# Two preactivated 3x3 convolutions on eight images: units of 12 rows of two images in 64x64 tiles against blocks of 16 rows of one image in 64x32 and 32x32 tiles

## The reference

```python
def _gn(v, G=4, eps=1e-5):           # group norm: 4 groups of 2 channels, whole image
    g = v.reshape(B_, G, C_ // G, H_, W_)
    m = jnp.mean(g, axis=(2, 3, 4), keepdims=True)
    s = jnp.var(g, axis=(2, 3, 4), keepdims=True)
    return ((g - m) / jnp.sqrt(s + eps)).reshape(v.shape)

# x: (8 images, 8 channels, 1024, 1024) fp32; weights (8, 8, 3, 3), bias (8,)
x = x + conv3x3(_gn(x), L0_conv_weight) + L0_conv_bias     # layer 0
x = x + conv3x3(_gn(x), L1_conv_weight) + L1_conv_bias     # layer 1
return x
```

## Time and profile before

| | |
|---|---|
| median of three runs | 4156.16 us |
| span of the profiled execution, first to last instruction | 4141.6 us |
| matmuls (PE) busy | 3666.7 us, 89% |
| weight loads (PEld) busy | 1715.4 us, 41% |
| DVE / ACT / POOL busy | 2025.6 / 1762.8 / 1360.0 us |
| moved by DMA | 1435.04 MB, mean 346 GB/s |
| granted clock of PE, mean | 0.983 |

### The profile page before, as it was taken

How to read it: one execution, slowest core, us unless ns; L and a number is a source line. 1 busy time by engine, 2 the same in 40 slices (tenths; PEclk the granted TensorE clock), 3 DMA queues, 4 the chain that set the end, 5 groups by cost and what they waited for, 6 DMA issues and landing times.

```text
span 4141.6 us, 88712 instructions
## 1 busy us (share of the span) xinstructions
PE 3666.7 (89%) x33232; PEld 1715.4 (41%) x33232; DVE 2025.6 (49%) x3110; ACT 1762.8 (43%) x1381; POOL 1360.0 (33%) x1829
## 2 busy tenths in 40 slices
PE   0087777898889999999888999999999999999999
PEld 0032222353334433354333443345444444566665
DVE  6866666665556344446656444444445322232222
ACT  0032222343334555543333555544443555555554
POOL 0011111121112555531111455552111455555555
PEclk9999998999999999999999999999999999999999
DMA  9989999999999999999999999999999999999997
GB/s 333 396 291 393 386 374 371 366 368 387 382 382 331 331 367 385 380 318 391 390 388 384 305 357 371 374 295 368 362 355 333 291 306 306 306 287 304 305 303 237
DMA packets 367109, 1435.04 MB, mean 346 GB/s; under 512 B 49888, under 2 KB 50016, under 8 KB 334176
## 3 DMA queue, kind: packets, MB, share of 16 engines
q10 hardware_dynamic: 176736, 627.30, 47.9%
q0 software_dynamic: 153344, 536.96, 34.5%
q1 hardware_dynamic: 36864, 268.45, 16.9%
HBM read 895.64 MB, written 536.87 MB: 346 GB/s over the span
## 4 chain that ended last, share of the span: by engine, by line
PE 56%; DMA 15%; ACTq 11%; issue 10%; DVE 5%; ACT 2%; DVEq 0%; POOL 0%; POOLq 0%; SPq 0%
PE conv L653 56%; DMA out_dram<-out_tile 12%; ACTq L479 11%; DMA stat_tile<-x_dram 2%; DVE bn_x L700 2%; ACT out_tile L465 1%; DVE bn_mid L710 1%; DMA mid_dram<-out_tile 1%; DVE out_tile L727 1%; DVE mv_mid L738 1%; DVEq L700 0%; DVE mv_x L732 0%; PE conv L555 0%; ACTq L461 0%; PE conv L583 0%
## 5 line engine op out<-in xcount | busy, mean ns | idle before, releaser
L653 PE MATMUL conv<-x_tile,wts 64*64 64x512 f32 x32832 | 3648.7, 598 | 235.5 <-ACT out_tile L465 140.4
L653 PEld LDWEIGHTS conv<-x_tile,wts 64*64 64x64 f32 x32832 | 1694.9, 134 | 2170.3 <-issue 2037.0
L465 ACT ACTIVATE out_tile<-conv,bias 128x1024 f32<-128x1024 f32 x688 | 728.6, 1110 | 1340.5 <-PE conv L653 791.1
L710 DVE BATCH_NORM_STATS2 bn_mid<-out_tile 128x512 f32 (+1 forms) x1376 | 849.3, 680 | 881.1 <-ACT out_tile L465 880.9
L727 DVE TENSOR_SCALAR out_tile<-conv,bias 128x1024 f32<-128x1024 f32 x340 | 436.4, 1284 | 1168.7 <-PE conv L653 856.7
L371 POOL DMA_DIRECT2D mid_dram<-out_tile x680 | 343.4, 507 | 1708.1 <-ACT out_tile L465 1641.4
L470 ACT ACTIVATE out_tile<-conv,bias 128x1024 f32<-128x1024 f32 x344 | 383.1, 1114 | 764.4 <-PE conv L653 505.6
L508 ACT ACTIVATE x_tile<-x_tile 16x2048 f32<-16x2048 f32 x340 | 648.6, 1908 | 44.9 <-issue 31.6
L700 DVE BATCH_NORM_STATS2 bn_x<-stat_tile 128x512 f32 (+1 forms) x1024 | 628.7, 678 | 45.6 <-DMA stat_tile<-x_dram 45.5
L405 POOL COPY x_tile<-x_tile 16x2048 f32<-16x2048 f32 x340 | 639.1, 1880 | 1.7
L385 POOL DMA_DIRECT2D out_dram<-out_tile x680 | 348.3, 514 | 823.7 <-DVE out_tile L727 758.8
(11 more groups left out here) (62 smaller groups left out, 114.5 us busy)
## 6 DMA issues: line engine op xcount, KB each, us to landing
x_tile<-x_dram ACTq DMA_DIRECT2D x680, 512.0 KB, 23.0
stat_tile<-x_dram SPq DMA_DIRECT2D x256, 1024.0 KB, 9.8
out_dram<-out_tile POOLq DMA_DIRECT2D x680, 384.0 KB, 7.8
mid_dram<-out_tile POOLq DMA_DIRECT2D x672, 384.0 KB, 9.3
x_tile<-mid_dram ACTq DMA_DIRECT2D x340, 640.0 KB, 6.4
x_tile<-mid_dram ACTq DMA_DIRECT2D x344, 128.0 KB, 8.5
mid_dram<-out_tile POOLq DMA_DIRECT2D x8, 416.0 KB, 10.0
x_tile<-x_dram ACTq DMA_DIRECT2D x8, 256.0 KB
```

Source lines behind the costliest of these rows:

```text
L465: last = act.activation(out_tile[0:parts, slot, i], conv[0:parts, bank, i], ACT.Identity, bias=bias0[0:parts, win.parity, int(unit.last), ...
L653: last = nc.tensor.matmul(to, weights, x_tile[HALF * half:HALF * (half + 1), slot, middle, c + kw:c + kw + BANK], start=(kw == 0), stop=(k ...
L710: last = dve.bn_stats(bn_mid[0:parts, unit.win.pair % 2, i, bass.ds(unit.n * 2 + h, 1), :] .rearrange("p a b -> p (a b)"), out_tile[0:part ...
```

## The change

The whole kernel body is written anew for another tiling.

* A *block* is 16 rows of one image, 16 rows x 8 channels = 128 partitions, and each input row is loaded once. A *unit* is two blocks (32 rows of one image), 32 units to a *pass* (one layer of one image), 16 passes: 512 units.
* The input block is shifted by one row against the output block (input rows 16b+1 to 16b+16 for output rows 16b to 16b+15). Four quarters of 4 output rows each (32 partitions) make up the output block. Two of them need only rows of one half of the input block: `whole`, a 64x32 tile. The other two need rows of two quarters: `split`, two 32x32 tiles, the upper of which may lie in the block before.
* A unit is 2 column halves x 3 `kw` x (4 `whole` + 8 `split`) = 72 matmuls of 512 columns. The 12 of one `kw` cover the array once.
* Passes run in plain order: layer 0 of image n, layer 1 of image n, layer 0 of image n+1. The sums of a pass are made between two passes, with one set of weights.
* ACT makes all evictions (one of 128 partitions and two of 64 for each unit, since the second block's halves are swapped in PSUM) and asks for rows behind them, for the units 3 and 4 on. There are 8 slots of one block each. At the fourth unit from a pass's end it also asks for a small transfer of padding rows and waits for it.
* No halos are copied, DVE evicts nothing, and POOL stores only (two transfers of 512 KB to a unit).
* The statistics of x are those of the next image, asked for by SP as units get done.

```diff
-PAIRS = IMAGES // 2
-RING = 4
-X_RING = 8
-ROWS_IN = 8
-ROWS_OUT = 6
+TILE = P // 4
+BLOCKS = SIDE // ROWS
+UNITS = BLOCKS // 2
+TRIP = 4
+TRIPS = UNITS // TRIP
+SLOTS = 2 * TRIP
+PASSES = 2 * IMAGES
...
+            def whole(parity, j, c, kw):
+                for i in range(2):
+                    for h in range(2):
+                        part = slice(HALF * h, HALF * (h + 1))
+                        nc.tensor.matmul(columns_of(parity, i, 2 * h + 1, c), wts[part, WHOLE, kw],
+                                         rows_of(HALF * h, HALF, 2 * j + i, c, kw),
+                                         start=(kw == 0), stop=(kw == KW - 1))
+
+            def split(parity, j, c, kw):
+                first, end = c == 0 and kw == 0, c == 1 and kw == KW - 1
+                for i in range(2):
+                    slot = 2 * j + i
+                    for h in range(2):
+                        part = slice(HALF * h, HALF * h + TILE)
+                        nc.tensor.matmul(columns_of(parity, i, 2 * h, c), wts[part, SPLIT, kw],
+                                         rows_of(HALF * h, TILE, slot, c, kw), start=first, stop=end)
+                        q = 1 if h else 3
+                        part = slice(TILE * q, TILE * (q + 1))
+                        above = slot if h else (slot - 1) % SLOTS
+                        last = nc.tensor.matmul(columns_of(parity, i, 2 * h, 1 - c),
+                                                wts[part, SPLIT, kw],
+                                                rows_of(TILE * q, TILE, above, 1 - c, kw),
+                                                start=first, stop=end)
+                return last
...
+                whole(parity, j, 0, 0)
+                split(parity, j, 0, 0)
+                whole(parity, j, 0, 1)
+                split(parity, j, 0, 1)
+                whole(parity, j, 0, 2)
+                split(parity, j, 0, 2).then_inc(half_added, 1)
+                whole(parity, j, 1, 0)
+                pe.wait_ge(half_added, UNITS * p + TRIP * t + (j + 1))
...
+            with pe.Fori(0, PASSES) as p:
+                sums(p)
+                pe.wait_ge(pads_written, p + 1)
+                pe.wait_ge(wts_ready, p + 1)
...
+            def load_last_pad(layer, n):
+                act.wait_ge(pad_row_filled, 2 * n + (layer + 1))
+                act.sem_inc(rows_asked)
+                act.dma_start(x_tile[P - CH:P, LAST_SLOT, 1:SIDE + 1], pad_row[0:CH, :]) \
+                    .then_inc(last_pad_loaded, 16)
...
+                if (g + TRIP - 1) % UNITS == UNITS - 1:
+                    load_last_pad(layer, n)
+                    load(TRIP, 0)
+                    act.wait_ge(last_pad_loaded, 32 * n + 16 * (layer + 1))
+                    act.sem_inc(rows_asked)
+                    load(TRIP - 1, 1)
                 else:
+                    load(TRIP - 1, 1)
+                    load(TRIP, 0)
...
+                act.activation(out_tile[:, slot, 0], conv[:, parity, 0], ACT.Identity,
+                               bias=bias[:, 0:1]).then_inc(evicted, 1)
+                act.activation(out_tile[HALF:P, slot, 1], conv[0:HALF, parity, 1], ACT.Identity,
+                               bias=bias[0:HALF, 0:1]).then_inc(evicted, 1)
+                act.activation(out_tile[0:HALF, slot, 1], conv[HALF:P, parity, 1], ACT.Identity,
+                               bias=bias[HALF:P, 0:1]).then_inc(evicted, 1)
+                load_next(n, g, last_image)
```

More of the change, by code:

```diff
@@ L11 @@
 P = 128
-HALF = P // 2
 CH = 8
@@ L156, in last_stores @@
[L156 to L169, removed]
+PER_GROUP = STATS * STAT_PARTS // GROUPS
+MID_PARTS = UNITS * 2 * HALVES
+STAT_UNITS = sorted(list(range(0, 60, 2)) + [31, 33])
@@ new lines, in image @@
+            def image(n, first_image=False, last_image=False):
+                for layer in range(2):
+                    act.wait_ge(var_read, 2 * n + (layer + 1))
+                    act.activation(root[:, :], var[:, :], ACT.Sqrt).then_inc(root_done, 1)
+                    act.wait_ge(wts_ready, 2 * n + (layer + 1))
+                    for u in range(UNITS):
+                        evict(n, layer * UNITS + u, first_image, last_image)
+            load_head(0, 0)
+            for b in range(LAST_SLOT):
+                load_block(0, 0, b)
@@ L549, in _ @@
+            image(0, first_image=True)
+            with act.Fori(1, IMAGES - 1) as n:
+                image(n)
+            image(IMAGES - 1, last_image=True)
         @block.tensor
         def _(pe):
-            def mean_sum(n, bank):
-                pe.wait_ge(mean_share, n + 1)
-                regions = 1 if WINDOWS[n].layer == 0 else 3
-                for region in range(regions):
-                    last = nc.tensor.matmul(conv[:, bank, 1, BANK:BANK + BOTH], average[:, :],
-                                            share[:, region], start=(region == 0),
-                                            stop=(region == regions - 1))
-                last.then_inc(mean_summed, 1)
@@ L560, in var_sum @@
-            def var_sum(n, bank):
-                pe.wait_ge(var_share, n + 1)
-                regions = 1 if WINDOWS[n].layer == 0 else 3
-                for region in range(regions):
-                    last = nc.tensor.matmul(conv[:, bank, 1, BANK:BANK + BOTH], average[:, :],
-                                            share[:, region], start=(region == 0),
-                                            stop=(region == regions - 1))
-                last.then_inc(var_summed, 1)
-            def own(i):
-                return slice(VALID * i, VALID * i + HALF)
@@ new lines, in rows_of, with columns_of @@
+            def rows_of(first, rows, slot, c, kw):
+                at = c * BANK + kw
+                return x_tile[first:first + rows, slot, at:at + BANK]
+            def columns_of(parity, i, quarter, c):
+                column = TILE * ((quarter + 2 * i) % 4)
+                return conv[column:column + TILE, parity, i, c * BANK:(c + 1) * BANK]
+            def whole(parity, j, c, kw):
+                for i in range(2):
+                    for h in range(2):
+                        part = slice(HALF * h, HALF * (h + 1))
+                        nc.tensor.matmul(columns_of(parity, i, 2 * h + 1, c), wts[part, WHOLE, kw],
+                                         rows_of(HALF * h, HALF, 2 * j + i, c, kw),
+                                         start=(kw == 0), stop=(kw == KW - 1))
@@ L854, in _, with make_bias @@
-            dve.memset(rows0[:, 0:KW, :], 0.0)
-            after_all(dve.memset(rows1[:, :, :, :], 0.0))
+                dve.wait_ge(head_loaded, 16 * (p + 1))
+                dve.tensor_scalar(x_tile[part, LAST_SLOT, 1:SIDE + 1], head[part, :],
+                                  is_first[part, 0:1], above[part, 0:1], ALU.mult, ALU.add) \
+                   .then_inc(pads_written, 1)
+            def make_bias(p, layer):
+                dve.wait_ge(bias_summed, p + 1)
+                dve.tensor_scalar(bias[:, :], conv[:, 0, 0, GROUPS:GROUPS + 1],
+                                  bias_col[:, layer:layer + 1], None, ALU.add).then_inc(wts_ready, 1)
@@ L949, in _taps @@
+            with dve.Fori(0, IMAGES - 1) as n:
+                image(n, False)
+            image(IMAGES - 1, True)
 def _taps(weight, np):
```

969 lines of the change are left out of this document (313 added, 656 removed).

## The result

The kernel after took **6574.1 us**, the kernel before 4156.5 us beside it (medians of four runs each): the ratio is 1.582, with a 95% interval from 1.5781 to 1.5861. One of the four runs after, 7669 us at a mean granted clock of 0.793, was disturbed and is left out of the ratio. The profiled execution took 6573.2 us, with a span of 6571.5. The forecast was 3761 us. The case that came true is rival 1, for which 6000 us were worked out.

A forecast was written before the change was run, and what follows sets the result against it. Half the kernel was taken as DMA-bound, half as PE-bound, with DMA the limit after: 127 start + 3452 DMA + 109 boundaries + 48 padding + 10 end = 3746 us span, plus 15 makes 3761 us; range 3560 to 4150.

The forecast's parts named there:

- rival 1: Tiles of two sizes do not run side by side on PE; a unit takes 10.4 to 11.6 us, 6000 us in all; 17%.
- Can the 12 tiles fill it?: PE's instruction pace: 144 record pairs must come in 5.2 us, 36 ns each; bounds 4.2 and 8.0 us a unit.
- PE's work: Conv matmuls: 512 units of 6 array covers at 5.21 us, 2668 us against 3584 before, 916 us less.
- the warm row: PE's warm stream before the change: 36 pairs of one column at 29 ns each, taken as the nearest price.
- The two records of another size: Beside the 128x128 sums on PE, two records of 8 columns push the next unit by 0.31 us, some 0.1 us a switch.
- Bytes: DMA traffic: 1342 MB against 1435, as the halo rows of layer 0 go.
- Start: First pass: one image's sums, aggregations and the chain to the first conv matmul; conv starts at 127 us, 228 before.
- ACT: Three evictions and two requests take 3.3 to 4.4 us of a unit, below 6.9, so no bound; costed at nothing.
- DMA's rate: Mixed traffic when DMA is the limit: 378 GB/s, weighted from four stretches at 369 to 388.
- Boundaries: Between passes PE idles 15.7 us (layer 0 to 1) or 8 us (1 to 0); DMA loses 109 us in all.
- The padding row: ACT's wait for a small transfer in each pass: 3 us of idle DMA in each of 16, 48 us; upper bound 160.
- The sum: The whole span: start, DMA-paced passes, boundaries, padding waits and end make 3746 us, plus 15 is 3761 us.

The follow-up runs named there:

- twelve tiles: The kernel with all tiles 32x32, but 12 of the 16 of each `kw`, half of each `whole` left out (another output): 3826.3 us.
- the last kernel: All tiles 32x32, ACT's image loop unrolled, DVE writes the padding row into the slot in place of the small transfer: 3853.5 us, ratio 0.9235 to the kernel before.
- experiment (c): On all tiles 32x32: padding transfer waited for one unit later, ACT's image loop unrolled, GpSimd fills the padding row after the weights: 3906.0 us, ratio 0.9364.
- (b): On the kernel with all tiles 32x32, ACT's loop over the images is unrolled: 3926.7 us, ratio 0.9416.

## Why the prediction was wrong

**The step that failed** is "Can the 12 tiles fill it?", and with it "*PE's work*": "512 units of 6 covers, if `whole` and `split` fill the array together". They do not. The forecast of PE's unit was 5.21 us, it took 12.06, and 512 x 6.85 = 3507 us are more than the whole miss of 2813 (DMA's waits, which the forecast had, are hidden behind PE now). The step looked for the price of a pair of instructions, between 29 and 56 ns, and took the warm row. That part held: with one size a `kw` of 24 pairs takes 0.86 us, 36 ns a pair, and one of 32 pairs 1.05, 33 ns. But all rows of overlap are of one size, and the sum went by them. The two records of another size spoke of 0.1 us for a change. The Trainium skill (TensorEngine Tiling (Array Packing), Key Properties), which rival 1 quotes, says that a change of the tiling mode drains the engine. Both pointed at rival 1, which got 17%.

**Rival 1** named the mechanism and undersized it: 6 x 1.74 = 10.4 us is right (10.31), a change is 0.146 us and not 0.1, so a unit is 12.06 and not 11.6. Over its upper end, 6280, that is 512 x 0.46 = 236 us. The 15 boundaries are 437 - 15 x 12.06 = 256 us instead of 190, 66 more. Together 6582. For 224 of the 256 us no conv matmul runs; the other 32 are the first units, 2 us too long each. In the first pass of layer 1 the granted clock is 0.50 (the 1.2 GHz level) for PE's first 5 us, from 533.6 to 538.6, after 17.8 us in which it had run the few matmuls of the sums only. No term of the sum had that. The signs that it named are all there: PE busy throughout, `whole` and `split` in groups, DMA at 216 to 220 GB/s.

The other steps, the second half of them by the kernels with equal tiles, as DMA isn't the limit after:

* *Bytes*: 1342 forecast, 1344.3 measured.
* *Start*: conv at 127 us. Its first matmul starts at 127.3, with 32x32 tiles at 125.0. Right.
* *ACT* at nothing: right. In the kernel after it idles 8.7 us in each unit, with 32x32 tiles 3.34, ended by PE both times.
* *DMA's rate*, 378 GB/s: 381 and 384 in the last kernel's stretches. Right for these, but it isn't the same whatever the mix: with twelve tiles the passes of layer 0 move 381 to 388 GB/s and those of layer 1 394 to 398, while layer 0 of the last image, which reads no statistics, has a share of 1.02 at 345.
* *Boundaries*: 15.7 us without PE from layer 0 to 1. Here they are in the timeline of the kernel after; the last eviction of the pass began at 515.9.

```profile
519.35 1.29 DVE L476 BATCH_NORM_STATS2 bn_mid<-out_tile 128x6 f32<-128x512 f32 x2 [0.98 <-ACT out_tile L341]
520.79 3.62 DVE L490 BATCH_NORM_AGGREGATE mv_mid<-bn_mid 128x2 f32<-128x768 f32 x1 [0.15 <-DVE bn_mid L476]
524.82 0.56 PE L367 MATMUL conv<-share,average 128*128 128x4 f32 x2 [9.00 <-DVE share L492]
...
528.07 2.90 POOL L243 TENSOR_SCALAR pad_row<-zeros,own_mean 8x1024 f32<-8x1024 f32 x1 [7.50 <-DVE own_mean L525]
528.22 0.99 DVE L531 TENSOR_SCALAR newton<-newton 128x4 f32<-128x4 f32 x1
...
530.01 1.08 DVE L541 TENSOR_SCALAR wts<-band,own_rstd 128x192 f32<-128x192 f32 x1
...
533.64 1.93 PE L395 MATMUL conv<-x_tile,wts 64*32 64x512 f32 x8 [2.55 <-DVE bias L562]
```

It took 17.7 us. Statistics (1.3) and aggregation (3.6) are as forecast; of the 2 us more, 1.5 are in the chain behind, where two of DVE's small instructions take 0.8 us longer beside GpSimd's fill (L243). With the fill moved behind the weights, experiment (c), the same instructions are short:

```profile
373.94 0.16 DVE L537 TENSOR_SCALAR newton<-newton 128x4 f32<-128x4 f32 x1
374.91 0.32 DVE L547 TENSOR_SCALAR wts<-band,own_rstd 128x192 f32<-128x192 f32 x1
...
377.13 2.83 POOL L243 TENSOR_SCALAR pad_row<-zeros,own_mean 8x1024 f32<-8x1024 f32 x1 [10.83 <-DVE bias L568]
```

From layer 1 to 0 PE stands for 8.2 to 8.3 us where ACT doesn't jump, as forecast. The jump of ACT's loop, 4 to 7 us at each of five of these boundaries, was in no term.
* *The padding row*: 3 us in each of 16 passes, 48 in all. With 32x32 tiles it is 8 to 10 us in the last three units of seven passes of layer 0 and none in the other nine. From (b) to the last kernel, which has no such wait, the passes are 56 us shorter together and the boundaries 10 (the fill is gone too). The total is near by luck: the price of a pass was too low by a factor of about three, and nine of the 16 passes pay nothing.
* *The sum*: the change as it was meant, with equal tiles and free of ACT's wait, its jump and the fill, has a span of 3855 us against 3746. It adds up as 128 at the start, 512 x 6.72 = 3441, 15 boundaries of 323 - 15 x 6.72 = 222, 55 of units over 6.72 and 10 at the end. The unit of 6.72 holds the pause at the wait for `half_added`, which no term had; what it would be without that wait wasn't run. The forecast had 109 for the boundaries, because PE at 5.2 us a unit would catch up what DMA's queue held ready. At 6.72 us PE has nothing to catch up with, and the boundaries count in full. That reading comes from the sum, no run tests it alone.

## What to carry to other kernels

Tiles of two sizes did not share TensorE's array in either pair tried, on columns of their own: count a unit as the sum of the rounds of each size, plus 0.15 us for each change. Where a design needs both, cut the larger tile into tiles of the smaller size that add up in two PSUM banks: a third more matmuls took this kernel from 6574 to 3970 us. Then look for waits in the stream of matmuls that the alternation had hidden: here one in each unit cost 0.4 us with 64x32 tiles and 0.7 with twelve 32x32. A rule that would turn the result round is to be given more weight than rows of overlap without its condition, here two sizes.

## What the runs showed of the hardware

* A change between 64x32 and 32x32 tiles costs 0.146 us (8 of them 1.17 us), one between 32x64 and 32x32 0.16, and in both pairs the two sizes exclude each other. A matmul record of 512 columns in fp32 is 0.43 us at a granted clock of 1.00.
* Sixteen 32x32 tiles side by side take 1.04 to 1.06 us for two records each, twelve take 0.86. So the full set has some 0.19 us over. Right behind the pause at the wait sixteen take 0.86 and 0.89 as well, so the array can do it; that the 64 instructions (16 by 2 weight loads and 2 matmuls) come too slowly otherwise is argued and not tested.
* ACT idles for 3.8 to 5.4 us at its jump back over a long loop body, and these boundaries are 4 to 7 us longer; unrolled, with five such jumps gone, it idles for 0.03 us there, and the span was 41 us shorter.
* A GpSimd `tensor_scalar` of 8x1024 (2.9 us) stretches two of the small DVE instructions beside it, 0.16 to 0.99 us and 0.32 to 1.08; those in between stay at 0.16 to 0.27.
* One core with reads and writes mixed moved 369 to 398 GB/s at a DMA share of 1.01 to 1.03 in the kernel before, the one with twelve tiles and the last, and 345 in one pass without statistics.
